# Three blocks of each down-weight split to ScalarE and VectorE, two to GpSimd, with an earlier second split and earlier loads

## The reference, cut to what matters

```
def _L0_ffn_ref(x, ln_gamma, ln_beta, gate_w, w1, w2):   # E=8, K=2, C=512, F=1024
    ...
    rn = (xf - mu) * jax.lax.rsqrt(var + EPS) * ln_gamma + ln_beta
    logits = rn @ gate_w.T
    probs = jax.nn.softmax(logits, axis=-1)
    rw, sel = jax.lax.top_k(probs, K)
    comb = jnp.sum(jax.nn.one_hot(sel, E, dtype=xf.dtype) * rw[..., None], axis=1)
    h = jax.nn.gelu(jnp.einsum('nc,efc->enf', xf, w1), approximate=False)
    y = jnp.einsum('enf,ecf->enc', h, w2)
    out = jnp.einsum('enc,ne->nc', y, comb)
```

## Time and profile before

| what | value |
|---|---|
| runs of the kernel before | median 934.28 us, 933.08 to 936.36 |
| the profiled execution's own time | 938.36 us |
| its span | 936.6 us |
| mixture, from the last attention instruction to the end | about 731 to 936.6 us |
| busy in the whole span | PE 94%, DVE 72%, ACT 56%, POOL 41% |
| bytes read from HBM | 95.03 MB |

### The profile page before, as it was taken

The page is one execution under the profiler, slowest core; times in us unless marked ns, Lnnn a source line. Parts: engine busy times, 40 slices in busy tenths (PEclk is TensorE's granted clock), DMA queues, the critical chain, the costliest instruction groups (busy, mean ns, idle before and its releaser), DMA issues. The chain is left out here.

```text
span 936.6 us, 24792 instructions
## 1 busy us (share of the span) xinstructions
PE 879.1 (94%) x10509; PEld 625.3 (67%) x10509; DVE 677.9 (72%) x1022; ACT 527.7 (56%) x811; POOL 387.2 (41%) x294
## 2 busy tenths in 40 slices
PE   5999999999999999999999999989888899998995
PEld 2565777776676776776867867755546787766663
DVE  7856787656688655688656556667778678989993
ACT  3644445565354564354565554552657278989893
POOL 1131775445576445566445555536230042111122
PEclk9999999999999999999999999999989999999999
DMA  9364122442121441221342211308414739999982
GB/s 341 119 170 117 27 68 60 135 125 76 41 70 39 121 134 37 60 57 47 82 125 80 70 38 33 93 2 304 171 54 164 284 126 361 406 401 401 400 280 34
DMA packets 48456, 134.69 MB, mean 144 GB/s; under 512 B 9894, under 2 KB 11814, under 8 KB 44494
## 3 DMA queue, kind: packets, MB, share of 16 engines
q1 hardware_dynamic: 45354, 126.81, 40.2%
q0 software_dynamic: 2800, 6.04, 3.2%
q10 hardware_dynamic: 192, 0.26, 0.1%
HBM read 95.03 MB, written 11.31 MB: 114 GB/s over the span
## 5 line engine op out<-in xcount | busy, mean ns | idle before, releaser
L472 POOL TENSOR_TENSOR acc_pool<-acc_pool,pT 128x1024 f32<-128x1024 f32 x90 | 212.0, 2356 | 146.3 <-ACT pT L742 144.7
L742 ACT ACTIVATE pT<-ps_s 128x1024 f32<-128x1024 f32 x124 | 126.9, 1023 | 196.5 <-PE ps_s L928 196.5
L578 DVE TENSOR_REDUCE mpart<-ps_b 128x1 f32<-128x512 f32 x256 | 173.4, 684 | 72.1 <-PE ps_b L908 71.3
L892 PE MATMUL ps_a<-wv_hi,cT_hi 128*128 128x128 f16 x1024 | 183.5, 219 | 0.0
L894 PE MATMUL ps_a<-wv_hi,cT_lo 128*128 128x128 f16 x1024 | 182.7, 219 | 0.0
L893 PE MATMUL ps_a<-wv_lo,cT_hi 128*128 128x128 f16 x1024 | 182.6, 219 | 0.0
L573 DVE TENSOR_TENSOR k_lo<-k_f,k_hi 128x512 f16<-128x512 f32 x64 | 76.4, 1194 | 58.1 <-ACT k_hi L715 58.1
L892 PEld LDWEIGHTS ps_a<-wv_hi,cT_hi 128*128 128x128 f16 x1024 | 99.8, 97 | 7.9 <-issue 6.0
L893 PEld LDWEIGHTS ps_a<-wv_lo,cT_hi 128*128 128x128 f16 x1024 | 100.2, 98 | 7.2
L894 PEld LDWEIGHTS ps_a<-wv_hi,cT_lo 128*128 128x128 f16 x1024 | 99.8, 97 | 0.0
L908 PE MATMUL ps_b<-k_stack,q_stack 101*128 101x512 f16 x256 | 96.8, 381 | 2.3 <-DMA k_stack<-k_lo 1.3
(11 more groups left out here) (290 smaller groups left out, 1855.5 us busy)
## 6 DMA issues: line engine op xcount, KB each, us to landing
w_raw<-in_w SPq DMA_DIRECT2D x30, 2048.0 KB, 17.0
raw<-in_context SPq DMA_DIRECT2D x16, 1024.0 KB, 6.2
k_stack<-k_hi SPq DMA_DIRECT2D x252, 64.0 KB, 2.0
k_stack<-k_lo SPq DMA_DIRECT2D x128, 64.0 KB, 2.0
slots_in<-a_zeros SPq DMA_DIRECT2D x1, 3855.0 KB, 13.7
rows_in<-slots_in SPq DMA_DIRECT2D x15, 257.0 KB, 17.2
q_stack<-k_stack SPq DMA_DIRECT2D x12, 128.0 KB, 2.4
x_sb<-in_x SPq DMA_DIRECT2D x2, 512.0 KB, 4.1
```

The lines of the kernel that those rows point to most:

```text
L472: nc.gpsimd.tensor_tensor(acc_pool[:, :], pT[:, 0, :] if p == 1 else acc_pool[:, :], pT[:, p % PT, :], ALU.add).then_inc(pool_add, 1)
L578: nc.vector.tensor_reduce(mpart[:, j, kb:kb + 1], bank_at(step)[:, :], AX.X, ALU.max).then_inc(p1_max, 1)
L742: nc.scalar.activation(pT[:, p % PT, :], scores(w, p)[:, :], ACT.Exp, scale=SM_SCALE).then_inc(exp_done, 1)
L892: nc.tensor.matmul(to, cT_hi[:, c, keys], t.wv_hi[:, c, col], start=(c == 0), stop=False)
```

## The change

The down weights of a tile are eight blocks of 512 columns. ACT and DVE now split the first six (two halves of three blocks), and POOL the last two in a function `w2_share` of three instructions, each waiting for the one ahead: raw times a constant in place (TENSOR_SCALAR), a copy into the float16 hi half (CAST), and lo = raw - hi (TENSOR_TENSOR), all 128 x 1024. This holds for tiles 1 to 14; tile 0 is split in the self-attention as before. A new semaphore `w2_pool` tells that they are done; `down_tile` and `w2_load` wait for it as well. To have a semaphore free, `row_out` of the cross-attention is merged into `bias_out`, with the counts adapted.

Further, w2 of tile 1 is split ahead of the loop (ACT) and in its first turn (DVE); `EARLY` is 4, so that the rows of tile 3 also come by products; and SP issues w2 of tile 3 and w1 of tile 5 ahead of the wait for the scatter and ahead of all rows.

```diff
-EARLY = 3
+POOL_BLOCKS = 2
+EARLY = 4
...
         def w2_split(w, i):
-            return w[:, NF // 2 * i:NF // 2 * (i + 1), :]
+            n = (NF - POOL_BLOCKS) // PARTS
+            return w[:, n * i:n * (i + 1), :]
+
+        def w2_pool_part(w):
+            return w[:, NF - POOL_BLOCKS:NF, :]
...
             def w2_load(k):
                 sp.wait_ge(w2_lo_s, w2_parts(k - 2))
+                sp.wait_ge(w2_pool, w2_pool_parts(k - 2))
...
             w1_load(4)
+            w2_load(3)
+            w1_load(5)
             sp.wait_ge(sent, 16 * 2 * NB)
             for k in (*range(EARLY, ROWS_AHEAD), *range(EARLY)):
                 rows_load(k)
             experts_of_further_tiles()
             for k in range(TILES):
-                if k + ROWS_AHEAD < TILES:
+                if EARLY <= k + ROWS_AHEAD < TILES:
                     rows_load(k + ROWS_AHEAD)
-                if 5 <= k + 4 < TILES:
+                if 6 <= k + 4 < TILES:
                     w1_load(k + 4)
-                if 3 <= k + 2 < TILES:
+                if 4 <= k + 2 < TILES:
                     w2_load(k + 2)
...
+            def w2_share(k):
+                u = k % 2
+                pool.wait_ge(w2_in[u], 16 * uses(k))
+                if k >= 2:
+                    pool.wait_ge(down, k - 1)
+                raw, hi, lo = [w2_pool_part(w[u]) for w in (w2_raw, w2_hi, w2_lo)]
+                nc.gpsimd.tensor_scalar(raw, raw, W_SCALE, None, ALU.mult).then_inc(w2_pool, 1)
+                pool.wait_ge(w2_pool, w2_pool_parts(k) - 2)
+                nc.gpsimd.tensor_copy(hi, raw).then_inc(w2_pool, 1)
+                pool.wait_ge(w2_pool, w2_pool_parts(k) - 1)
+                nc.gpsimd.tensor_tensor(lo, raw, hi, ALU.subtract).then_inc(w2_pool, 1)
+
             pool.wait_ge(s.out_sem, 16 * (NB + 1))
+            w2_share(1)
             for k in range(TILES):
+                if k + 2 < TILES:
+                    w2_share(k + 2)
                 pool.wait_ge(y_out, k + 1)
...
+            w2_low(1, (0,))
             for k in range(TILES):
...
+                    if (k, i) == (0, 0):
+                        w2_low(1, (1,))
...
-                if k:
+                if k >= 2:
                     w2_low(k)
...
+            w2_high(1)
             x_high(0)
...
             def down_tile(k):
                 pe.wait_ge(h_lo_s, 2 * (k + 1))
                 pe.wait_ge(w2_lo_s, w2_parts(k))
+                if k:
+                    pe.wait_ge(w2_pool, w2_pool_parts(k))
```

More of the change, by code:

```diff
@@ L308, in cross_attention @@
         x_tr, x_tr_hi, x_tr_lo = sem("x_tr"), sem("x_tr_hi"), sem("x_tr_lo")
-        bias_mm, row_out, bias_out = sem("bias_mm"), sem("row_out"), sem("bias_out")
+        bias_mm, bias_out = sem("bias_mm"), sem("bias_out")
         q_mm, q_out, q_hi_s, q_lo_s = sem("q_mm"), sem("q_out"), sem("q_hi_s"), sem("q_lo_s")
@@ L653, in bias_row_out @@
                 act.wait_ge(bias_mm, 2 * n + 1)
-                nc.scalar.activation(bias_row[n], bias_bank(n)[0][0:1, :], ACT.Copy).then_inc(row_out, 1)
+                nc.scalar.activation(bias_row[n], bias_bank(n)[0][0:1, :], ACT.Copy).then_inc(bias_out, 1)
             def bias_columns_out(i):
@@ L660, in bias_columns_out @@
                                      scale=A_SCALE if i == 2 else 1.0).then_inc(bias_out, 1)
-                act.wait_ge(bias_out, n + 1)
+                act.wait_ge(bias_out, 2 * n + 2)
             def queries_out(g):
@@ L789, in bias_in_a_row @@
                 if n == 1:
-                    pe.wait_ge(row_out, n)
+                    pe.wait_ge(bias_out, 2 * n - 1)
                 if n == 2:
@@ L799, in bias_columns @@
                 n = BIASES.index(i)
-                pe.wait_ge(row_out, n + 1)
-                if n:
-                    pe.wait_ge(bias_out, n)
+                pe.wait_ge(bias_out, 2 * n + 1)
                 for g in range(NG):
@@ L871, in _ @@
                             pe.wait_ge(w_lo, 3)
-                            pe.wait_ge(bias_out, 2)
+                            pe.wait_ge(bias_out, 4)
                     bank, col, keys = bank_at(step[:3]), slice(P * g, P * (g + 1)), slice(KB * kb, KB * (kb + 1))
@@ L1553, in mixture @@
                                                  sem("m_y_out"))
-        y_added, copied = sem("y_added"), sem("m_copied")
+        y_added, copied, w2_pool = sem("y_added"), sem("m_copied"), sem("m_w2_pool")
         def w1_split(w, i):
@@ L1559, in w2_split, with w2_pool_parts @@
         def w2_split(w, i):
-            return w[:, NF // 2 * i:NF // 2 * (i + 1), :]
+            n = (NF - POOL_BLOCKS) // PARTS
+            return w[:, n * i:n * (i + 1), :]
+        def w2_pool_part(w):
+            return w[:, NF - POOL_BLOCKS:NF, :]
+        def w2_pool_parts(k):
+            return 3 * k
         def uses(k):
@@ L1782, in w1_low, with w2_low @@
                                                    op1=ALU.subtract).then_inc(w1_lo_s, 1)
-            def w2_low(k):
-                for i in range(PARTS):
+            def w2_low(k, parts=range(PARTS)):
+                for i in parts:
                     v.wait_ge(w2_hi_s, w2_parts(k - 1) + i + 1)
```

## The result

The changed kernel took 965.19 us (median of 4 runs, 959.93 to 967.46), the kernel before 935.32 us beside it: a ratio of 1.030, 95% interval 1.023 to 1.037. The profiled execution took 967.46 us with a span of 965.7, 29.1 us more than before's 936.6. I compare the two traces by the spans.

The account below looks back on a forecast made before the run. Transfers bound the kernel at 11.69 us a tile, DVE 0.88 behind. Late start plus ten 13.3 us tiles put tile 14's transposes 25.6 us later: 964 profiled, 960 us predicted from the 934.28 median, range 942 to 985.

Parts of the forecast that it names:

- The hold: Steady tile: POOL's share holds DVE, 2.22 plus twice 0.96 less 0.4 over 9.60, giving 13.3 us a tile.
- The second rival: Steady tile: only the subtraction holds DVE, 11.4 us, below transfers' 11.69; late start remains, 944 us; chance 0.07.
- the third: Rival for the tile loop: nothing holds DVE and POOL's time is hidden; about 936 us, no change; chance 0.04.
- the fourth: Rival at the start: nothing holds DVE and tile 0's rows pass the weights, landing by about 776; 929 us; chance 0.06.
- these instructions exclude each other for their whole length: Tile loop: POOL's instructions and DVE's with two SBUF inputs shut each other out; only about 0.14 us is saved.
- the first rival: Steady tile: one-input POOL instructions are dear, 1.6 to 2.36 us each; 14.7 to 15.9 a tile, 975 to 988; chance 0.13.
- The start: Before the steady tiles: tile 0's rows wait behind POOL's first share and 4 MB of weights; tile 4's transposes 9.5 us late.
- ACT's wait: Sign of being right, ahead of `y_evict` of tile 0: ACT waits over 15 us for the rows.
- the short end of the two I had: Start: rows' landing after the first weight load, 13.6 us from load sizes against 17.1 seen; 15.5 was taken.
- The end: After tile 14's transposes: no change, with DVE's last split 1.1 us shorter but POOL's adds queued behind its share.
- Behind it I change nothing: After tile 14's transposes at 929.9, the time to the end was left as in the kernel before.
- the sum: Whole chain: 796.9 + 10 x 13.3 = 929.9 for tile 14's transposes against 904.31, 25.6 us later.

Follow-up runs that it names:

- e6: Changed kernel with POOL's multiplication and conversion kept and its subtraction dropped: 947.34 us, ratio 1.012 to the kernel before.
- e9: Changed kernel with only the multiplication left of POOL's three instructions: 938.49 us, ratio 1.001 to the kernel before.
- e4: Changed kernel with POOL's three instructions replaced by six memsets of the same part of w2's raw buffer: 944.71 us, ratio 1.008 to the kernel before.
- e3: Changed kernel with the rows' loads of tiles 0 to 3 issued ahead of w2(3) and w1(5): 956.80 us, ratio 1.023 to the kernel before.
- e2: Kernel before plus POOL's share alone, without early split, early loads or fourth tile by products: 957.77 us, ratio 1.022 to the kernel before.
- e1: Changed kernel without POOL's share, ACT and DVE splitting all eight w2 blocks: 950.07 us, ratio 1.013 to the kernel before.
- e5: Changed kernel with only the subtraction left of POOL's three instructions: 941.59 us, ratio 1.008 to the kernel before.

## Why the prediction was right

The range of 942 to 985 us around the forecast of 960 held 965.19. The mechanism, DVE held by POOL and rows held behind the first share, is the one that the runs show; that the sizes came out so close is in part luck. The steps:

- **The hold.** Forecast 3.74 us a tile over DVE's own 9.60 (0.96, 0.96 and 2.22, less 0.4), measured 3.6 over about 9.5 (0.84, 0.83 and 1.94); 13.3 us a tile against 13.16. The second rival (only the subtraction holds) falls with e6 and e9, the third (nothing holds) with the trace itself, the fourth (rows past the weights by 776 us) with 788.72; e4 shows that it is the hold and not POOL's time.
- **A step that was wrong inside it:** "these instructions exclude each other for their whole length", with 1.1 us for the multiplication. It takes 2.77 us alone. With the three times measured alone, as the prediction counts, the tile should have taken some 14.7 us, the first rival's low end. It did not hold DVE for its whole length but for 0.84 us in most tiles of this trace. Price and rule were both off for the multiplication, in opposite directions, and that they cancelled is luck. The conversion (1.04 for 1.1) and the subtraction (2.13 for 2.36) were priced well and kept the rule: they hold for their own time less 0.2 us, where the prediction took off 0.14.
- The Trainium skill ("SBUF — State Buffer", section "SBUF: two separate sides") has the rule of the whole instruction, too, and says that a two-input VectorE instruction meets only GpSimd instructions that read SBUF. The second half agrees with e4's memsets (3.43 and 4.49 us undisturbed); the first agrees with the conversion and the subtraction, but not with 0.84 us of hold by a multiplication of 2.77.
- **The start.** Rows of tile 0 forecast at 788.1, tile 0 written at 788.72; ACT's wait, over 15 us by the forecast, was 20.33. Two errors cancelled: the first share ended at 775.04 rather than 772.6 (the dear multiplication, and the conversion, which waited through both w1 splits: 4.16 us for 1.04), and the rows followed 13.6 us after w2(3), the short end of the two I had. Behind it I had left out that the first h_lo is held as well (2.97 for 0.68 us), and put the clock into the range only: PE ran at 0.50 until 798 us (its up product of tile 3, 794.26 to 801.7, took 7.4 us for 5.56). Tile 4's transposes came at 801.7, not 796.9.
- **The end.** "Behind it I change nothing" was wrong by 1.8 us: the adds that queue behind the share of tile 14, which the prediction named, were not made up for by DVE's shorter last split.
- Against the profiled execution I had 964 us; it took 967.46. The start gave 4.8 us more, the ten tiles 3.1 less, the end 1.8 more.
- **What the sum hid:** it added start and tiles. e3 shows that they overlap: 15.4 us at tile 4's transposes were worth 12.0 us between the profiled executions and 8.4 between the medians, since with DVE as the bound an earlier PE only waits later. And the share alone cost 20 us in e2 (957.77 against 938.01), rather than the 16 of ten tiles at 1.6: DVE is held from the first tiles on, and a part of it comes due behind the last transposes. The 20.5 us of e4 hold more than that: its tile 0 was written 6 us earlier (782.74), and its tile is PE's 10.98.

## What to carry to other kernels

Work given to an idle GpSimd was not free here: its instructions that read SBUF held VectorE's splits, which take two operands from SBUF. Look first for one place in the trace where the two have met, and count the hold on the engine that would become the bound. A load that is moved ahead in a queue passes its wait on to everything behind it and its traffic to every small transfer in flight, so ask of each early load which short transfer is needed first. A delay read at one engine's instruction is worth at the end only what the bound engine loses by it.

## What was not expected of the hardware

- The multiplication (2.77 us alone) held DVE for 0.84 us where it started ahead of the split beside it and for 1.5 to 2.3 where it started behind the split's start, while the conversion (1.04) and the subtraction (2.13) held for about their own time. Why the multiplication differs stays open.
- DVE's `pick_rows`, four instructions of 128 x 128 to float16 that each read one tile and a column of scalars from SBUF, took 3.25 us in place of 0.87 when it met the first multiplication (765.43 above; 0.87 at 763.44 in e1), and the split behind them started some 1.2 us late. Memsets, which only write, stretched them too (2.46 us in e4). So not only two-input instructions are held; a conversion from PSUM never was.
- POOL was not always let in between two splits that followed each other directly: its conversion at 768.66 lasted until DVE's w1 pair was through, and in e5 one subtraction took 7.67 us. In the steady tile it was let in between them: the conversion at 877.77 ends at 880.68, within the pair of w1.
- Beside 2 MB weight loads, indirect DMAs land late: scatters 9 to 10 us in e1, where the last one before took 3.98 us; adds up to 21.78 us.
